# A spectral filter on stacked real and imaginary rows, in tiles of 48 channels instead of 96

## What is computed

```python
xf = jnp.fft.rfft2(x.astype(jnp.float32), axes=(1, 2), norm='ortho')
xf = xf.reshape(B, H, Wf, NB, BS)          # NB = 8 blocks of BS = 24 channels, Wf = 25
...
outr = einsum('bxyki,kio->bxyko', ar, wr) - einsum('bxyki,kio->bxyko', ai, wi) + b[..., 0]
outi = einsum('bxyki,kio->bxyko', ai, wr) + einsum('bxyki,kio->bxyko', ar, wi) + b[..., 1]
...                                        # layer 1, then relu; layer 2, then softshrink(., 0.01)
out = jnp.fft.irfft2(full.reshape(B, H, Wf, C), s=(H, W), axes=(1, 2), norm='ortho')
return out.astype(x.dtype) + bias
```

## Time and profile before

| | |
|---|---|
| time, median of three runs | 1100.19 us |
| the profiled execution's own time | 1095.46 us |
| its span | 1093.7 us |
| what lies around the span | 1.76 us |
| PE busy over the span | 1020.2 us (93%) |
| DVE, ACT, POOL busy | 856.6, 701.1, 146.5 us |
| granted TensorE clock, mean | 0.966 |

### The profile page before, as it was taken

How to read it: one execution, slowest core, us unless ns; L and a number is a source line. 1 busy time by engine, 2 the same in 40 slices (tenths; PEclk the granted TensorE clock), 3 DMA queues, 4 the chain that set the end, 5 groups by cost and what they waited for, 6 DMA issues and landing times.

```text
span 1093.7 us, 35778 instructions
## 1 busy us (share of the span) xinstructions
PE 1020.2 (93%) x15498; PEld 720.9 (66%) x15498; DVE 856.6 (78%) x1744; ACT 701.1 (64%) x1003; POOL 146.5 (13%) x118
## 2 busy tenths in 40 slices
PE   5978698999999999999999999999988989998998
PEld 3555155766767676777777767777657776785665
DVE  4869687989999999999999999999626765132564
ACT  4766076777878787777777777777774543231654
POOL 4530002900000000000000000000024454000111
PEclk9975599999999999999999999999999999999999
DMA  4797889466666565656656566656400100222221
GB/s 121 201 233 205 296 161 166 75 116 106 108 102 115 93 112 94 109 98 108 98 102 105 102 106 104 104 87 98 71 23 1 46 23 24 56 65 71 79 88 55
DMA packets 87970, 112.80 MB, mean 103 GB/s; under 512 B 14333, under 2 KB 80194, under 8 KB 87621
## 3 DMA queue, kind: packets, MB, share of 16 engines
q1 hardware_dynamic: 87783, 110.49, 51.2%
q10 hardware_dynamic: 30, 0.02, 0.0%
HBM read 86.82 MB, written 23.21 MB: 101 GB/s over the span
## 4 chain that ended last, share of the span: by engine, by line
PE 74%; DVE 11%; DMA 6%; ACT 4%; issue 3%; POOL 2%; SPq 0%; DVEq 0%; ACTq 0%
PE ps L1083 38%; PE ps L1242 18%; PE ps L1078 14%; DVE mx_p L1543 2%; DVE stage_lo L1512 2%; DVE xh L101 2%; ACT hid_f L1010 2%; POOL rstd L109 2%; DVE stats L88 1%; PE ps L1096 1%; DMA qv<-m_d 1%; DMA m_d<-mneg 1%; PE ps L1189 1%; ACT hid L1004 1%; DMA xin<-in_x 1%
## 5 line engine op out<-in xcount | busy, mean ns | idle before, releaser
L1543 DVE TENSOR_REDUCE mx_p<-ps 128x1 f32<-128x464 f32 (+1 forms) x1080 | 608.5, 629 | 40.3 <-PE ps L1083 30.4
L960 ACT ACTIVATE prob<-ps 128x768 f32<-128x768 f32 x648 | 495.9, 810 | 190.8 <-PE ps L1083 190.1
L1083 PE MATMUL ps<-kc,qc 112*32 112x464 f16 (+1 forms) x4320 | 462.8, 370 | 7.8 <-issue 3.4
L1083 PE MATMUL ps<-qv,ka 113*32 113x384 f16 x5184 | 405.1, 327 | 15.5 <-DMA qv<-m_d 10.4
L1242 PE MATMUL ps<-prob,v_ext 128*32 128x384 f32 x2592 | 293.7, 486 | 4.2 <-issue 3.4
L1083 PEld LDWEIGHTS ps<-qv,ka 113*32 113x32 f16 x5184 | 215.3, 97 | 91.5 <-issue 33.1
L1083 PEld LDWEIGHTS ps<-kc,qc 112*32 112x32 f16 x4320 | 174.7, 95 | 106.0 <-DVE mx_p L1543 26.9
L1242 PEld LDWEIGHTS ps<-prob,v_ext 128*32 128x32 f32 x2592 | 117.4, 110 | 19.0 <-issue 5.5
L1078 PE MATMUL ps<-xnt_all,w_up 96*128 96x384 f16 x432 | 75.0, 326 | 2.8 <-ACT hid_f L1010 2.8
L1078 PE MATMUL ps<-w_dn,hid 128*96 128x192 f16 (+1 forms) x756 | 68.2, 249 | 6.7 <-DVE hid L1598 4.4
L1078 PEld LDWEIGHTS ps<-w_dn,hid 128*96 128x96 f16 (+1 forms) x756 | 63.7, 114 | 12.0 <-issue 6.1
(11 more groups left out here) (109 smaller groups left out, 839.1 us busy)
## 6 DMA issues: line engine op xcount, KB each, us to landing
qv<-rel_d SPq DMA_DIRECT2D x216, 144.0 KB
qv<-kq_d SPq DMA_DIRECT2D x108, 216.0 KB
qc<-rel_d SPq DMA_DIRECT2D x22, 216.0 KB, 4.2
xin<-in_x SPq DMA_DIRECT2D x12, 288.0 KB, 3.7
kq_d<-khl SPq DMA_DIRECT2D x24, 144.0 KB, 2.8
q_h<-kq_d SPq DMA_DIRECT2D x9, 288.0 KB, 4.8
q_w<-qw_d SPq DMA_DIRECT2D x9, 288.0 KB, 6.9
rel_d<-stage_hi SPq DMA_DIRECT2D x4, 648.0 KB, 10.7
```

The costliest lines, as they stand in the source:

```text
L960: nc.scalar.activation(prob[:, s4(p, s), :].rearrange("p (a b) -> p a b", a=2), ps[:, 3 + 2 * (s % 2):5 + 2 * (s % 2), 0:CW], ACT.Exp).the ...
L1083: ins = nc.tensor.matmul(ps[c:c + 32, bank, 0:w], l[:, c:c + 32], r, start=True, stop=True, tile_position=(0, c))
L1543: nc.vector.tensor_reduce(mx_p[:, q * GT + k // MP, k % MP:k % MP + 1], ps[:, slot, 0:min(MW, N - k % MP * MW)], AX, ALU.max).then_inc(uni ...
```

## The change

The channels are worked on in FG = 4 tiles of FC = 48 (two blocks of 24) instead of 2 of 96, and real and imaginary parts are stacked on the partitions, real at 0 to 47 and imaginary at FR = 64 to 111 (FP = 112 partitions in all). FN = 480 is two tiles x 5 frequencies x 48 positions.

- `transform`: for each tile and frequency two matmuls of 48 columns, the real part at array column 0 and the imaginary part at 64: 40 instead of 10 of 96 columns.
- `layer1`: the weights hold the whole complex matrix over 112 partitions, so 4 matmuls of 240 columns stand where 8 stood.
- `layer2`: 40 matmuls of 48 columns, in pairs at array columns 0 and 64, instead of 20 of 96. `f_r` and its two DVE instructions go.
- `inverse`: 2 matmuls of 480 columns.
- In group 0 the matmuls of `transform` and `layer2` have 64 output rows instead of 48, so that the rows between the two parts are written once.
- The order on PE becomes `layer1(g)`, `transform(g+1)`, `inverse(g-1)`, `layer2(g)`, and on ACT `f_transformed(g+1)` comes ahead of `f_inverse(g-1)`.
- DVE adds the second bias in one instruction; POOL spreads it into `f_b2` at the end of `block0`, and clears three narrow pads there. At the start of the kernel POOL clears three more tiles.
- `load_transforms` issues nine DMAs instead of six. In head 3, `swap_filters` copies weight rows on chip by two DMAs, and ACT negates two pieces ahead of head 10 instead of one.

The diff, without declarations of tiles and semaphores:

```diff
@@ loads of constants (SP) @@
-            load(eng, f_b1[:, :, :].rearrange("p r k -> p (r k)"), d["f_b1"].rearrange("r (k p) -> p (r k)", p=C2))
+            eng.wait_ge(fw_zero, 4)
             for r in range(2):
-                load(eng, f_b2[r * S:(r + 1) * S, :], d["f_b2"][r:r + 1, :].to_broadcast([S, C]))
+                load(eng, dft_hi[r * FR:r * FR + S, :], d["c_dft_h"][r * S:(r + 1) * S, 1, :])
+                load(eng, f_b1[r * FR:r * FR + FC, :], d["f_b1"][r:r + 1, :].rearrange("o (g p) -> p (o g)", p=FC))
+                load(eng, f_b2s[r * FR:r * FR + S, :], d["f_b2"][r:r + 1, :].to_broadcast([S, C]))
...
+        def swap_filters(eng):
+            eng.wait_ge(consts, NCONST[0])
+            for r in range(2):
+                load(eng, f_w[FR:FP, :, :, r, 0:FC].rearrange("p l g c -> p (l g) c"),
+                     f_w[0:FC, :, :, 1 - r, 0:FC].rearrange("p l g c -> p (l g) c"))
...
+                    if is_at(n, 3) and q == 1:
+                        swap_filters(sp)
@@ POOL @@
             norm_root(pool, nc, rstd, ln1, 1)
+            nc.gpsimd.memset(dft_hi[:, :], 0.0).then_inc(fw_zero, 1)
+            nc.gpsimd.memset(f_b1[:, :], 0.0).then_inc(fw_zero, 1)
+            nc.gpsimd.memset(f_b2s[:, :], 0.0).then_inc(fw_zero, 1)
...
             chunks(block0)
+            for b in range(2):
+                nc.gpsimd.memset(f_in[:, b, KG * C:KG * C + FPAD], 0.0)
+            nc.gpsimd.tensor_copy(f_b2[:, :, :, :], f_b2s[:, :].rearrange("p (g c) -> p g c", g=FG).unsqueeze(2)
+                                  .to_broadcast([FP, FG, KG, FC])).then_inc(f_b2_ok, 1)
             skip(NC - 1)
+            nc.gpsimd.memset(f_a[:, 2 * FN:2 * FN + FPAD], 0.0).then_inc(f_pads, 1)
@@ ACT @@
+                for j in range(FG):
+                    w = KG * S
+                    ins = nc.scalar.activation(f_a[:, j * w:(j + 1) * w],
+                                               ps[0:FP, 2 + j // 2, j % 2 * w:(j % 2 + 1) * w],
+                                               ACT.Relu, bias=f_b1[:, j:j + 1])
                 ins.then_inc(fa_ok, 1)
+                if g + 1 < G:
+                    f_transformed(g + 1)
                 if g > 0:
                     f_inverse(g - 1)
-                if g + 1 < G:
-                    f_transformed(g + 1)
@@ PE @@
-                for k in range(2):
+                for j in range(FG):
                     for f in range(KG):
-                        ins = mm(ps[0:C2, k, f * 2 * S:(f + 1) * 2 * S], f_in[:, g % 2, f, k * C2:(k + 1) * C2],
-                                 dft_h[:, 0, :])
+                        M = FC if g else FR
+                        x = f_in[:, g % 2, f * C + j * FC:f * C + j * FC + M]
+                        col = j % 2 * KG * S + f * S
+                        for r in range(2):
+                            ins = nc.tensor.matmul(ps[r * FR:r * FR + M, j // 2, col:col + S], x,
+                                                   dft_h[:, 0, r * S:(r + 1) * S], start=True, stop=True,
+                                                   tile_position=(0, r * FR))
...
+                for j in range(FG):
+                    cols = slice(j % 2 * KG * S, (j % 2 + 1) * KG * S)
+                    ins = mm(ps[0:FP, 2 + j // 2, cols],
+                             f_w[:, 0, j, :, :].rearrange("p r c -> p (r c)")[:, 0:FP], f_x[:, j // 2, cols])
...
+                        for r in range(2):
+                            ins = nc.tensor.matmul(ps[r * FR:r * FR + M, 4 + j // 2, col:col + FC], x,
+                                                   f_w[:, 1, j, r, 0:FC], start=True, stop=True,
+                                                   tile_position=(0, r * FR))
...
+                for a in range(2):
+                    ins = mm(ps[0:2 * S, 6 + a, 0:FN], dft_hi[:, :], f_o[:, a, :])
...
+            pe.wait_ge(f_pads, 1)
             transform(0)
             for g in range(G):
                 layer1(g)
+                if g + 1 < G:
+                    transform(g + 1)
                 if g > 0:
                     inverse(g - 1)
-                if g + 1 < G:
-                    transform(g + 1)
                 layer2(g)
@@ DVE @@
-                nc.vector.tensor_scalar(f_r[:, :, :, 0, :], f_a[:, :, :, 1, :], -1.0, None, ALU.mult)
-                nc.vector.tensor_copy(f_r[:, :, :, 1, :], f_a[:, :, :, 0, :]).then_inc(fr_ok, 1)
...
+                nc.vector.tensor_tensor(f_y[:, :, :], ps[0:FP, 4:6, 0:FN],
+                                        f_b2[:, :, :, :].rearrange("p (a g) f c -> p a (g f c)", a=2),
+                                        ALU.add).then_inc(fy_ok, 1)
```

More of the change, by code:

```diff
@@ L67 @@
 G = KF // KG
+FC = 2 * BS
+FG = C // FC
+FR = 64
+FP = FR + FC
+FN = FG // 2 * KG * S
+FPAD = FR - FC
 EPS = 1e-5
@@ L212, in build @@
             hid_f = sb("hid_f", [128, HM, CW], F32, r)
[L213 to L218, removed]
+        f_x = sb("f_x", [FP, 2, FN])
+        f_a = sb("f_a", [FP, 2 * FN + FPAD])
+        f_y = sb("f_y", [FP, 2, FN])
+        f_c = sb("f_c", [FP, 2, FN])
+        f_o = sb("f_o", [FP, 2, FN])
         f_u = sb("f_u", [2 * S, KG, C])
+        f_b2 = sb("f_b2", [FP, FG, KG, FC])
         h1 = sb("h1", [T, CT, C])
@@ L225, in build @@
         xnt_f = sb("xnt_f", [C2, 2, CW])
[L226 to L227 removed]
+        f_in = sb("f_in", [2 * S, 2, KG * C + FPAD])
         at_t = sb("at_t", [C2 + 1, 2, CW])
@@ L991, in _ @@
             wait_consts(act)
-            nc.scalar.activation(f_wn[:, :, :], f_w[:, 0, :, 1, :], ACT.Copy, scale=-1.0).then_inc(fw_neg, 1)
+            for layer in range(2):
+                ins = nc.scalar.activation(f_w[FR:FP, layer, :, 0, 0:FC], f_w[FR:FP, layer, :, 0, 0:FC], ACT.Copy,
+                                           scale=-1.0)
+            ins.then_inc(fw_neg, 1)
             period(NH - 2, 0)
@@ L1037, in f_transformed @@
                 wait_used(act, f1_ps, g)
-                nc.scalar.activation(f_x[:, :, :, :, :].rearrange("p a k r h -> p a (k r h)"),
-                                     ps[0:C2, 0:2, 0:KG * 2 * S], ACT.Copy).then_inc(fx_ok, 1)
+                nc.scalar.activation(f_x[:, :, :], ps[0:FP, 0:2, 0:FN], ACT.Copy).then_inc(fx_ok, 1)
             def f_inverse(g):
@@ L1409, in layer1 @@
                 wait_used(pe, fa_ok, g)
[L1410 to L1415, removed]
+                for j in range(FG):
+                    cols = slice(j % 2 * KG * S, (j % 2 + 1) * KG * S)
+                    ins = mm(ps[0:FP, 2 + j // 2, cols],
+                             f_w[:, 0, j, :, :].rearrange("p r c -> p (r c)")[:, 0:FP], f_x[:, j // 2, cols])
                 ins.then_inc(f1_ps, 1)
             def layer2(g):
[L1419 to L1423, removed]
-                        mm(o, f_a[:, k, f, :, :].rearrange("p r h -> p (r h)"), f_w[:, 1, k, 0, :], stop=False)
-                        ins = mm(o, f_r[:, k, f, :, :].rearrange("p r h -> p (r h)"), f_w[:, 1, k, 1, :],
-                                 start=False)
+                pe.wait_ge(fa_ok, g + 1)
+                wait_used(pe, fy_ok, g)
+                for j in range(FG):
+                    for f in range(KG):
+                        col = j % 2 * KG * FC + f * FC
+                        M = S if g else FR
+                        x = f_a[:, j * KG * S + f * S:j * KG * S + f * S + M]
+                        for r in range(2):
+                            ins = nc.tensor.matmul(ps[r * FR:r * FR + M, 4 + j // 2, col:col + FC], x,
+                                                   f_w[:, 1, j, r, 0:FC], start=True, stop=True,
+                                                   tile_position=(0, r * FR))
                 ins.then_inc(f2_ps, 1)
@@ L1430, in inverse @@
                 pe.wait_ge(fo_ok, g + 1)
-                for j in range(-(-KG // 2)):
-                    w = min(2, KG - 2 * j)
-                    ins = mm(ps[0:2 * S, 4 + j, 0:w * C], dft_h[:, 1, :],
-                             f_o[:, 2 * j:2 * j + w, :].rearrange("p f c -> p (f c)"))
+                wait_used(pe, fu_ok, g)
+                for a in range(2):
+                    ins = mm(ps[0:2 * S, 6 + a, 0:FN], dft_hi[:, :], f_o[:, a, :])
                 ins.then_inc(fi_ps, 1)
```

49 lines of the change are left out of this document (22 added, 27 removed).

## The result

| | before | after |
|---|---|---|
| median of the runs, us | 1098.6 (1096.81 to 1101.25, 4 runs) | 1088.38 (1083.43 to 1092.73, 4 runs) |
| ratio | | 0.9919 [0.9893, 0.9945] |
| the profiled execution, us | 1095.46 | 1092.73 |
| core: first `transform` to last `f_u`, us | 58.84 | 54.44 |

The forecast was 1093.3. The time came out faster and inside the range, but by another sum: the core gave back half of what was predicted (4.4 us of 8.8), and the rest of the gain lies outside the core, where the prediction had only costs. The two profiled executions differ by 2.7 us only, the medians by 10; that too needs an explanation, and gets it at the end.

The account below looks back on a forecast made before the run. PE was taken to bound the core's middle, 10.14 us a group. Core -10.5, POOL's copy +1.0, head 1's DMAs +0.9 and clock +1.7 gave -6.9 us, from 1100.19 to 1093.3; range 1086 to 1101.

Parts of the forecast that it names:

- The block of pairs: `transform` and `layer2` on PE: paired matmuls overlap, 1.70 us a block, 1.80 with the switch, 2.10 in group 0.
- my path: Chain of waits through the core, first `transform` to last `f_u`: 48.3 us against 58.8, so -10.5, without the clock's cost.
- The serial rival: `transform` and `layer2`: pairs don't overlap, 3.40 us a block, 3.50 with steps; 1104.6 us in all; chance 0.18.
- The two stalls: PE idle 2.3 us each ahead of `transform(3)` and `transform(4)`, because their loads are issued behind stores on SP.
- sign of being wrong: Prediction wrong if pair blocks take over 2.5 us, stalls exceed 3 us, or the clock stays at 0.50 beyond one stretch.
- The clock: PE in the core: half clock may follow each stall, up to 1.7 us each; one taken, +1.7, range 0 to 3.4.
- POOL's copy: End of `block0`: spreading the bias on POOL slows DVE's normalisation; +1.0 us taken, between 0 and 1.2.
- Head 1's DMAs: Attention, head 1: three more DMAs on SP delay the bias row for head 2; +0.9 us taken, between 0 and 1.3.

Follow-up runs that it names:

- e2: Changed kernel with 13 matmuls that nobody reads ahead of `transform(3)` and `transform(4)`: 1086.8 us, ratio 0.9896 to the kernel before, core 49.86 us.
- e3: Changed kernel with all real parts of a `transform` or `layer2` block first, then all imaginary ones: 1101.42 us, ratio 1.0035 to the kernel before.
- e1: Changed kernel with all loads of the core ahead of the stores on SP: 1081.07 us, ratio 0.9847 to the kernel before, core 45.10 us.
- e6: Changed kernel with the second bias spread by four ACT copies instead of POOL's copy: 1091.13 us, ratio 0.991 to the kernel before.
- p2: Changed kernel with 32 unused bytes a partition ahead of attention's tiles: 1101.47 us, ratio 1.0019 to the kernel before.
- e0: Changed kernel run again with no edit: 1089.93 us, ratio 0.9933 to the kernel before, core 54.73 us.
- e4: Changed kernel with `inverse` ahead of `transform` on PE and ACT, as before the change: 1086.18 us, ratio 0.9873 to the kernel before, core 48.94 us.

## Why the prediction was right, and where it was not

*The block of pairs*: right in kind, a little low. The rows were misread in part: the short matmuls of the earlier trace rows are twelve (24 records, one of them behind the x23) on three column tiles, not sixteen, so one after the other they would take 0.71 us instead of 0.95, still twice the 0.34 measured; and the change alternates two column tiles with the whole array, not four. 1.84 to 1.94 instead of 1.80, and 2.43 instead of 2.10 in group 0. The core without the clock's part comes to 49.86 (e2) against 48.3 by my path, and these blocks are most of the 1.6; the wait for group 4's load, longer by 0.5, is the next. The serial rival had its price right (3.59 against 3.50), and its sign: e3.

*The two stalls*: right. 2.13 and 2.44 instead of 2.3 each, for the reason given; 4.8 us by e1 and e2, against 4.6. Over all profiles that have them they are 1.93 to 3.55; the longest, in e6, is past the 3 us that the prediction had named as a sign of being wrong.

*The clock*: the step that failed most. I took one half-clock stretch out of two, 1.7, and had both, 3.4, as the end of the range; it is 4.6 by e2, because the clock falls behind both stalls and one of the two stretches lasts twice as long as the other (6.8 and 3.4 us, in all five profiles that have both stalls); why it does stays open. A clock at 0.50 beyond one stretch was itself a sign of being wrong by the prediction. The 3.4 came from the one stretch of the earlier trace rows, where the clock recovered after 3.3 us.

*POOL's copy*: 1.0 taken, 0.3 measured. The copy is faster than scaled from the earlier trace rows (0.98 instead of 1.4), and most of DVE's 0.73 had cover.

*Head 1's DMAs*: 0.9 taken. A wait of 1.78 us shows up where it was looked for, but not in every profile (e3, e6), and on attention's end no cost can be told.

*What no step had*: attention. Between the means of three and nine profiles it ends 807.9 - 803.3 = 4.6 us earlier, and 4.4 of that is there by the sixth store to `m_d` (253.4 against 249.0). The change makes the constants 672 bytes larger and so moves attention's tiles. p2 shows that such a move can cost more than this; that it is the cause here is likely but not shown. I had searched the change for instructions and transfers, and a tile's size is neither.

The sum, on ordinary executions: core 54.6 - 58.84 = -4.2, POOL +0.3, attention -4.6, together -8.5; the medians say -7.0 (e0) and -10.2. Predicted were -8.8, +1.0, +0.9: -6.9. From the last `f_u` to the end all profiles take 97.3 to 98.1, so nothing else hides there. A core gain that was overrated by 4.6 us (2.9 by the clock, the rest mostly by the blocks) and a gain of 4.6 us in attention that no step had cancelled each other: the total came out right by luck, and it is no proof of the steps. In the two profiled executions the difference is only 2.7, because before's was 2.1 quicker than usual in `block0`, and after's attention ended 2.9 later than the mean of the nine.

## What to carry to other kernels

When blocks in a pipeline get shorter, follow every load that stands behind a store on its queue, and move it in the same edit: here the order on SP cost 9.5 us of the 13.7 that the shorter blocks were worth. A stall of 2 us ahead of the bound engine is to be priced with what the clock does behind it, about as much again here. And before a small change of time is put down to the code, compare a place that the code doesn't touch: a tile that grows moves all tiles behind it, and 32 bytes of such a move cost p2 more than 9 us.

## What was not expected of the hardware

- Pairs of matmuls of 48 columns on two column tiles that share all rows, each with its own load of weights, take 1.84 us for 80 records, 23 ns each; the same 80 one tile after the other 3.59, 45 ns.
- With 64 weight columns instead of 48 the pairs take 2.43, and about 4.5 unpaired: the price goes up with the weight columns, though the moving columns are the same.
- Two idle times of 1.9 to 3.6 us on PE gave half clock for 10.2 us in all (6.8 behind one, 3.4 behind the other) in all five profiles that had them; four of 1.34 (e4) gave none.
- 32 bytes in the start address of SBUF tiles changed the DMA engines' time for the same bytes by 6 to 7% (49.0 to 49.8% of the span against 52.1).
